# Layer three of the bias network over four pairs of steps at a time, with a ring of eight second-layer outputs

## The reference

```python
pos = grid_q[:, :, None, :] - grid_kv[:, None, :, :]
bias = jnp.sign(pos) * jnp.log1p(jnp.abs(pos))
bias = jax.nn.relu(bias @ cpb_w1 + cpb_b1)      # 2 -> 64
bias = jax.nn.relu(bias @ cpb_w2 + cpb_b2)      # 64 -> 64
bias = (bias @ cpb_w3 + cpb_b3).reshape(b, GROUPS, H * W, Hd * Wd)   # 64 -> 1
sim = jnp.einsum('bhid,bhjd->bhij', qh, kh) + bias
attn = jax.nn.softmax(sim, axis=-1)
```

## Time and profile before

| | us |
|---|---|
| runs shown | 1540.26, 1541.29, 1541.89 (median 1541.29) |
| the profiled execution's own time | 1542.36 |
| its span | 1540.2 |
| bias network, first to last layer three | 104.13 to 979.10 |

### The profile page before, as it was taken

The page is one execution under the profiler, slowest core; times in us unless marked ns, Lnnn a source line. Parts: engine busy times, 40 slices in busy tenths (PEclk is TensorE's granted clock), DMA queues, the critical chain, the costliest instruction groups (busy, mean ns, idle before and its releaser), DMA issues.

```text
span 1540.2 us, 32924 instructions
## 1 busy us (share of the span) xinstructions
PE 1441.7 (94%) x12718; PEld 634.1 (41%) x12718; DVE 1098.4 (71%) x1788; ACT 960.3 (62%) x1169; POOL 512.1 (33%) x571
## 2 busy tenths in 40 slices
PE   3179999999999999999999999979999899999998
PEld 1132222222222222222222222454445588888885
DVE  6867777777777777777777777751003899999995
ACT  2546666666666666666666666433120599999995
POOL 5232222222222222222222222230000177777773
PEclk8569999999999999999999999999999999999999
DMA  1130000000000000000000000000001622222211
GB/s 63 46 106 2 1 2 1 1 1 1 1 2 1 1 1 1 1 2 1 2 1 1 2 1 1 1 1 0 0 0 51 223 60 65 63 59 54 54 27 54
DMA packets 16152, 37.00 MB, mean 24 GB/s; under 512 B 4170, under 2 KB 7626, under 8 KB 15917
## 3 DMA queue, kind: packets, MB, share of 16 engines
q1 hardware_dynamic: 16032, 35.46, 7.9%
q10 hardware_dynamic: 12, 0.01, 0.0%
HBM read 24.57 MB, written 10.89 MB: 23 GB/s over the span
## 4 chain that ended last, share of the span: by engine, by line
PE 81%; DVE 12%; issue 3%; ACT 1%; POOL 1%; DMA 1%; SPq 0%; DVEq 0%; ACTq 0%; POOLq 0%
PE ps L832 31%; PE ps L840 16%; PE ps L824 9%; DVE aneg L714 4%; PE ps L996 4%; PE ps L1004 4%; PE ps L945 4%; PE ps L955 4%; PE ps L988 2%; DVE conv L577 2%; PE ps L979 1%; DVE big L717 1%; PE ps L932 1%; PE ps L967 1%; PE ps L1054 1%
## 5 line engine op out<-in xcount | busy, mean ns | idle before, releaser
L621 DVE TENSOR_SCALAR big<-ps 128x512 f32<-128x512 f32 x1032 | 644.5, 687 | 238.7 <-PE ps L824 238.7
L440 ACT ACTIVATE big<-ps,vec 128x1024 f32<-128x1024 f32 x514 | 563.6, 1115 | 321.7 <-PE ps L832 321.7
L832 PE MATMUL ps<-big,w 64*64 64x512 f32 x4112 | 549.1, 604 | 0.0
L335 POOL TENSOR_TENSOR mv<-sx,sy 128x1024 bf16<-128x1024 bf16 x130 | 248.4, 1911 | 644.4 <-PE ps L824 643.7
L840 PE MATMUL ps<-big,w3s 128*32 128x512 f32 x2048 | 272.8, 605 | 0.0
L832 PEld LDWEIGHTS ps<-big,w 64*64 64x64 f32 x4112 | 133.1, 133 | 310.0 <-DVE big L621 216.0
L376 POOL TENSOR_TENSOR big<-BT,big 128x512 f16<-128x512 f32 x129 | 150.4, 1166 | 249.8 <-DVE big L717 249.8
L824 PE MATMUL ps<-mv,wl 60*64 60x512 bf16 x2064 | 209.3, 391 | 1.9 <-ACT vs L435 1.1
L824 PEld LDWEIGHTS ps<-mv,wl 60*64 60x64 bf16 x2064 | 62.0, 105 | 282.3 <-DVE big L621 280.9
L714 DVE TENSOR_REDUCE aneg<-ps 128x1 f32<-128x1024 f32 x131 | 158.3, 1209 | 5.6 <-PE ps L988 5.4
L495 ACT ACTIVATE big<-ps,aneg 128x1024 f32<-128x1024 f32 x130 | 149.1, 1147 | 5.7 <-DVE aneg L714 5.1
(11 more groups left out here) (128 smaller groups left out, 949.0 us busy)
## 6 DMA issues: line engine op xcount, KB each, us to landing
h1h<-q_d SPq DMA_DIRECT2D x64, 128.0 KB, 2.9
h1l<-k_d SPq DMA_DIRECT2D x64, 128.0 KB, 3.1
q_d<-XN SPq DMA_DIRECT2D x8, 512.0 KB, 2.6
k_d<-XN SPq DMA_DIRECT2D x8, 512.0 KB, 2.6
X<-in_x SPq DMA_DIRECT2D x2, 1024.0 KB, 6.3
out<-X SPq DMA_DIRECT2D x8, 256.0 KB, 2.0
m<-grid_d SPq DMA_DIRECT2D x1, 1024.0 KB, 4.7
m<-in_m1T SPq DMA_DIRECT2D x1, 1024.0 KB, 5.9
```

Source lines behind the costliest of these rows:

```text
L335: pool.tensor_tensor(mv[i][:, :].rearrange("p (a b) -> p a b", a=H), sx[:, g, jj, :].unsqueeze(1).to_broadcast(shape), sy[:, g, jj, :].uns ...
L440: act.activation(h2[m % HRING], z2[m % 2], ACT.Relu, bias=v("cb2")).then_inc(h2_ready, 1)
L621: dve.tensor_scalar(h1[m % HRING][:, HALF * a:HALF * (a + 1)], z1[n % 3], 0.0, None, ALU.max).then_inc(h1_ready, 1)
L832: last = pe.matmul(z2[m % 2][CH * a:CH * (a + 1), HALF * r:HALF * (r + 1)], w2[CH * r:CH * (r + 1), :], h1[m % HRING][CH * r:CH * (r + 1), ...
```

## The change

Layer three runs once in four steps instead of once in two, and then over four pairs: two calls of `layer3` stand behind each other where `i % 4 == 3`. To keep four more outputs of the second layer until then, the `h2` ring gets eight places (rows 0 to 3 and 8 to 11 of `big`; `h1` keeps 4 to 7). `l3_done` now counts bursts of four pairs: ACT's wait before place `m % 8` is for the burst that read pair `m - 8`. The waits before `layer2` and `layer1` ask for the same counts as before, written with a helper `by_dve`. The number of matmuls, of ReLUs and of copies stays as it was.

```diff
-HRING = 4
+HRING, H2RING, BURST = 4, 8, 4
...
-        h2 = [big[:, i, :] for i in range(HRING)]
+        h2 = [big[:, i + i // 4 * 4, :] for i in range(H2RING)]
...
             def relu2(m):
-                act.activation(h2[m % HRING], z2[m % 2], ACT.Relu, bias=v("cb2")).then_inc(h2_ready, 1)
-
-            act.sem_inc(l3_done, 1)
+                act.activation(h2[m % H2RING], z2[m % 2], ACT.Relu, bias=v("cb2")).then_inc(h2_ready, 1)
+
...
             for g in range(G):
-                for m in range(AHEADQ, PAIRS + AHEADQ):
-                    act.wait_ge(z2_ready, PAIRS * g + m + 1)
-                    act.wait_ge(l3_done, PAIRS // 2 * g + m // 2)
+                for i in range(PAIRS):
+                    m = PAIRS * g + i + AHEADQ
+                    act.wait_ge(z2_ready, m + 1)
+                    if m >= H2RING:
+                        act.wait_ge(l3_done, m // BURST - 1)
                     relu2(m)
...
-                dve.wait_ge(l3_done, PAIRS // 2 * g + PAIRS // 2 + 1)
+                dve.wait_ge(l3_done, PAIRS // BURST * (g + 1))
                 dve.tensor_copy(BT[:, g, :], zb).then_inc(bias_saved, 1)
...
-                                     h2[(m + k // 2) % HRING][:, HALF * (k % 2):HALF * (k % 2 + 1)],
+                                     h2[(m + k // 2) % H2RING][:, HALF * (k % 2):HALF * (k % 2 + 1)],
                                      start=(m == 0), stop=(m == PAIRS - 2))
-                last.then_inc(l3_done, 1)
+                return last
...
                 for i in range(PAIRS):
-                    m = i + AHEADQ
-                    pe.wait_ge(h1_ready, 2 * PAIRS * g + 2 * m + 2)
-                    pe.wait_ge(h2_ready, PAIRS * g + m - 1)
+                    m = PAIRS * g + i + AHEADQ
+                    pe.wait_ge(h1_ready, by_dve(m))
+                    pe.wait_ge(h2_ready, m - 1)
                     layer2(m)
-                    pe.wait_ge(h1_ready, 2 * PAIRS * g + 2 * m + (4 if i + AHEAD1 == PAIRS else 3))
+                    if i + AHEAD1 == PAIRS:
+                        pe.wait_ge(h1_ready, by_dve(m + 1))
+                    else:
+                        pe.wait_ge(h1_ready, by_dve(m) + 1)
                     layer1(i + AHEAD1, g)
-                    if i % 2 == 1:
-                        pe.wait_ge(h2_ready, PAIRS * g + i + 1)
-                        if i == 1:
+                    if i % BURST == BURST - 1:
+                        pe.wait_ge(h2_ready, m - 1)
+                        if i == BURST - 1:
                             pe.wait_ge(bias_saved, g + 1)
-                        layer3(i - 1)
-
+                        for n in range(i - BURST + 1, i, 2):
+                            last = layer3(n)
+                        last.then_inc(l3_done, 1)
```

More of the change, by code:

```diff
@@ L849, in _, with by_dve @@
             pe.wait_ge(v_saved, 2)
+            def by_dve(m):
+                return 2 * (m + 1)
             for m in range(2):
@@ L854, in _ @@
             for m in range(AHEADQ):
-                pe.wait_ge(h1_ready, 2 * m + 2)
+                pe.wait_ge(h1_ready, by_dve(m))
                 layer2(m)
-                pe.wait_ge(h1_ready, 2 * m + 3)
+                pe.wait_ge(h1_ready, by_dve(m) + 1)
                 layer1(m + 2, 0)
```

## The result

| | before | changed |
|---|---|---|
| median of the runs | 1541.59 us (4 runs, 1540.26 to 1542.59) | 1556.61 us (4 runs, 1555.16 to 1558.51) |
| the profiled execution's own time | 1542.36 | 1555.72 |
| span | 1540.2 | 1553.9 |
| first to last layer three | 104.13 to 979.10 | 104.08 to 992.02 |
| one layer three to the next, mean | 3.431 for two pairs | 6.992 for four pairs |

The changed kernel takes 1.0099 times as long, with a 95% interval of 1.0081 to 1.0116: 15 us slower, forecast 18, inside the range.

The account below looks back on a forecast made before the run. PE, busy for 94% of the span, was taken as the bound. Each period for four pairs goes from 6.86 to 7.00 us, 128 x 0.14 = 18 us, so 1541.3 + 18 = 1559; 8-in-10 range 1549 to 1569.

Parts of the forecast that it names:

- The saving: Tile-shape changes around layer three: one visit fewer per four pairs saves 0.32 us, 128 times, 41 us.
- The wait of the third layer two: Third layer two after a burst waits 0.39 us for DVE's second ReLU half, starting 2.69 after the first.
- The rest of the table: Forecast PE starts over four steps and the burst, from the first layer two to the next at 7.00 us.
- the case for 12 us: Waiting layer two's weight load costs nothing more, 0.86 instead of 0.91: period 6.95, 12 us slower.
- 24 to 31: Layer two's two semaphores cost 0.10 instead of 0.05, delaying the third layer two and burst: 24 to 31 us slower.
- The sum: Period for four pairs 7.00 against 6.86 us: 128 x 0.14 = 18 us slower; half a microsecond at the stage's end.
- The covers: Costed at nothing: ACT's ReLUs, with cover of 0.4 us before layer two, and moving POOL's `spread` a step.
- Only the change of shape counts: Rival: the waits for DVE do not appear or other slack takes them up; 1500 us, chance 0.07.
- warning on emptying PSUM: Rule that emptying PSUM may become the bottleneck; as DVE's rate, 4.80 for 4.28 us over four steps, 26 us slower.
- half as long: Rival: the two new layer-two waits total 0.24 instead of 0.47 us; 12 us faster, 1530, chance 0.04.
- cancel: Rival: the waits are 0.14 us shorter in sum, leaving the time within 3 us, chance 0.07.
- those two rivals: DVE's halves each cost 0.69, 1593 us, chance 0.05; PE's clock falls, stage far over 100 us longer, chance 0.02.

Follow-up runs that it names:

- the two cut kernels: Changed kernel with first- and second-layer ReLUs over half their columns: layer three once in four steps 1472.64 us, once in two steps 1508.84 us.
- the two cuts: Changed kernel with only the second layer's ReLUs on ACT halved, 1558.21 us; with only the first layer's ReLUs on DVE halved, 1505.25 us.
- the two reorderings: Changed kernel with layer one issued three steps ahead instead of two, 1533.99 us; with layer one ahead of layer two in every step, 1524.66 us.
- the DVE cut: Changed kernel with each first-layer ReLU on DVE over 256 of its 512 columns: 1505.25 us, period 6.586.
- the two kernels with the delay taken away: Changed kernel with layer one three steps ahead and z1 banks rotating on, 1518.93 us; with layer one ahead of layer two and the copy on ACT, 1520.63 us.
- the first reordering: Changed kernel with layer one issued three steps ahead of its layer two instead of two: 1533.99 us, ratio 0.9955 to the kernel before.
- the kernel with the ring alone: Changed kernel with the h2 ring of eight kept but layer three back to once in two steps: 1541.50 us against 1541.38 for the kernel before.

## Why the prediction was right

- **The saving.** Forecast 0.32 us for each visit, 41 us in all; measured by the two cut kernels 0.293, 36 us. The 0.13 before layer three was 0.02 too high: that layer one had been waited for and loaded its weights late, and the 0.34 carried this too. Without the wait the two stand at 0.33 and 0.22.
- **The wait of the third layer two.** Forecast at 2.69 after the first, 0.39 late; measured 514.14 - 511.45 = 2.69, and 0.38 late. Adding up four rows of a kernel in which the wait did not exist gave the place to a hundredth. That it is DVE and not ACT, the two cuts show; that its delay is what makes the changed kernel slower than the one before, the two reorderings.
- **The rest of the table.** Forecast starts 0, 0.91, 1.12, 2.09, 2.69, 3.60, 3.89, 4.80, 5.14, 7.00; measured 0, 0.91, 1.13, 2.10, 2.69, 3.60, 3.90, 4.81, 5.14, 6.99. The late weights of 0.05 for each waiting layer two were paid (0.91 to the next layer one, both times), so the case for 12 us did not come about; the release by DVE stayed at 0.05, so neither did the case for 24 to 31.
- **The sum.** 128 x 0.13 = 16.6, not 18, from 0.01 of rounding in each period. At the end of the stage 0.68 was lost and not 0.5, 17.3 in all, against 15.0 between the medians (12.5 to 17.9 by the interval). The two profiled executions are 13.7 apart in span: 12.97 from the first to the last layer three and 0.68 behind it. Of the 16.6 the rest, 3.6, does not show, because the changed kernel's first layer three, issued two steps later, still came at 104.08 against 104.13: in its execution the granted clock had risen to 1.00 for good at 98 us, in the other only at 102. That scatter of some microseconds is greater than what was left to explain.
- **The covers.** ACT was not waited for, as said, and was next as said (the DVE cut). Its first ReLU ends at 512.61 + 1.115 = 513.73, 0.41 ahead of the third layer two, where 0.4 was forecast; but it lets a layer two go only 0.14 after its end, so the cover in use was 0.27. POOL's `spread` was never waited for.
- **The rivals.** "Only the change of shape counts" gave 1500. It is what the prediction made of the Trainium skill's rule that a change of tiling mode drains the engine (TensorEngine Tiling (Array Packing), Key Properties). The runs here agree that the change costs time, 0.29 us for a visit, but it was not all that counted. The Trainium skill's warning on emptying PSUM (TensorEngine Tiling (Array Packing), PSUM Bottleneck), taken as one on rates, was priced at 26 us; measured 15. That price was worked out wrongly: it added the 0.52 to a period of 6.86 that already holds two waits of 0.11 for DVE. Without counting them twice it is 6.86 - 0.32 - 0.22 + 0.52 = 6.84, no loss. Rate alone is what the two kernels with the delay taken away show: 6.69 and 6.71, faster than before by 0.15 to 0.17. It holds the gain down to about half of the 0.29 but does not make the loss. The two new waits were 0.46 together, against 0.47 forecast, so they were neither half as long nor did it cancel. DVE's halves stayed 0.60 apart, and the granted clock at 1.00, so those two rivals fell as well.

One thing was right only by care that a later step lacked: in the prediction I looked at which step the copy at a group's end fell on, and in the first reordering I did not look at which step the branch at a group's end fell on.

## What to carry to other kernels

A stage of work on the busiest engine can be a cover: before it is gathered into larger pieces, add up the delay of each path through the other engines and see whether what remains between producer and consumer still spans it. If not, the gain of gathering needs more distance along with it: here neither one alone gave anything (1540 us or slower), and both together, once the special steps at a group's end were mended, gave some 20 us. What can be won is then bounded by the rate of the next engine within the stretch, which its share of busy time does not show: here 0.36 of the 0.66 us of waiting in a period stayed. Steps that are special once in a loop, such as a bank that starts anew or a copy at a group's end, have to be looked at again after every shift, since they are hidden only where they happen to lie.

## What was not expected of the hardware

TensorE's granted clock rose at another time in each execution, and the execution's time moved with it. The kernel before and the kernel with the ring alone have the same code up to the bias network. In the profile of the first the granted clock was 0.50 (1.2 GHz) from 31 to 102 us and then 1.00 (2.4 GHz); in that of the second it was at 1.00 for most of the time from 87 to 93 us, fell again, and rose for good at 99:

```profile
87.00:93.00 6.00, 4.13 (x52) 3.78 (x54) 1.31 (x1) 1.38 (x4) 0.22 (x1) 0.50 0.58 193
93.00:97.00 4.00, 2.13 (x20) 0.78 (x18) 1.29 (x2) 1.26 (x4) 0.00 (x0) 0.50 1.06 388
```

```profile
87.00:93.00 6.00, 3.19 (x60) 2.46 (x60) 0.57 (x1) 2.63 (x7) 1.75 (x1) 0.95 0.79 278
93.00:97.00 4.00, 3.82 (x24) 1.16 (x28) 2.78 (x6) 1.11 (x1) 0.00 (x0) 0.50 1.05 395
```

The columns are the window, its length, busy us of PE, PEld, DVE, ACT, POOL with their instructions, granted clock, DMA share and GB/s. The first layer three came at 104.13 and at 101.03 us. PE's work ahead of it was small matmuls with waits between them, alike in both. Why the clock rose in one and not in the other was not tried. Runs of one and the same kernel show it too: of 17 runs of the kernel before on one chip, the four fastest (1537.48 to 1538.02 us) had a mean granted clock of 0.976, the slowest (1543.78) had 0.970. So a difference of 3 us takes many runs, where the period from the trace tells 0.01 us in 3.43 from a single one.
